# Layer 2 of a two-layer vision tower: the masked key copies of both halves of the heads on the scalar engine alone

## The chip, the cores and the metric

The kernel runs on one core of one Trainium2 chip. The time is device microseconds (us), the median of the runs. TensorE (PE), VectorE (DVE), the scalar engine (ACT), GpSimd (POOL) and the DMA queues (SP issues most of them) run side by side, each with its own instruction stream in program order, and meet at semaphores.

## The reference

The input is 32 images of 96 x 96 x 3. Patches of 16 x 16 become 36 tokens of 192 features, and a class token makes 37. Then come four blocks, each followed by a residual sum and a layer norm: attention with 12 heads of 16 features; a soft mixture of 64 experts; a second attention with two score maps; a second expert block. The change is in the second attention alone:

```
q = (x @ Wq).reshape(B, N, 2, H, D)      # 2 maps, 12 heads of 16
k = (x @ Wk).reshape(B, N, 2, H, D)
v = (x @ Wv).reshape(B, N, H, D)
out = softmax(q0 k0 / 4) v - exp(lambda) * softmax(q1 k1 / 4) v
h = layernorm(h + out @ Wo + bo)
```

## The kernel before, in words

**Tiling.** The 32 images go through the attention in four steps, called quads here: 8 images each, as 4 pairs (`QP = 4`, `QUADS = 4`). A pair lies on 101 partitions: one image on rows 0 to 36, the other on rows 64 to 100. The 192 features lie in two halves of 96 (`FH`), six heads each (`HH`). Times of 444 us to 640 us of the profiled execution are the second attention: quad 0 to about 495 us, quad 1 to 541, quad 2 to 587, quad 3 after that.

**Why there are masked copies.** For one pair, one map and one half, the scores of six heads come from one product: the stationary side is q of the half (96 features x 37 tokens), the moving side is K with 6 x 37 columns. So that a column belongs to one head alone, K is stored six times, each time with the features of all other heads put to zero. This masked copy is `k * hmask[:, h]`, read from PSUM, 96 partitions x 296 elements (8 images x 37 tokens) into `k_heads`. A quad of the second attention has 2 maps (m), 2 halves (mc) and 6 heads: 24 copies. The half mc = 0 is copied by ACT in `act_q` (L447), the half mc = 1 by VectorE in `dve_k` (L457), 12 copies each in every quad.

**What PE does in a quad** (`step` of `l1_pe`, L885). First q and K of map 1 (`pe_qk`, L353) into banks 4 to 7, for which it waits until the residual of the quad before (L961) has read banks 4 and 5. Then V (`pe_v`, L370) into banks 2 and 3. K of map 0 stood there, so `pe_v` waits for the copies of map 0. Then `pe_attention`: for each of eight units u (4 pairs x 2 maps), scores (L388), a turn of the probabilities (L399) and the product with V (L415); the first scores (u = 0) wait for all 24 masked copies. Between unit 0 and unit 1 it turns the normed output of the quad before (L880). Then, for the next quad, the turn of its input (L334), and of this quad's output (L552); q and K of map 0 of the next quad (L353, banks 0 to 3), and last the output projection of this quad (L905).

**What ACT does.** `act_q(1)`: two copies of q (L442) and the masked K of map 1; then for each unit the exp (L490) and the copy of turned probabilities (L497); copies of turned tiles (L344, L560); and `act_q(0)` of the next quad.

**What VectorE does** (`l1_dve`, L922). `dve_k` of map 1, the scaling of the layer norm of the quad before (`ln_scale`, L579), then per unit the row maximum (L480), the subtraction (L485) and the normalising (L520 to L533); the V copies (L474) between unit 1 and unit 2. At the quad's end `start(it + 1)`: its part of the turned input (L344) and `dve_k` of map 0 of the next quad; then the residual (L961, one piece for each half of the projection), and the moments of the norm (L571, L574), from which GpSimd makes the inverse deviation (L586).

**Order.** The order on each engine is as written in these functions. `maps` is 1 in the first layer and 2 in the second; `act_q`, `dve_k` and `pe_scores` serve both.

Of the kernel before, what the change touches and what calls it, by code (L numbers as in the profile page):

```python
# [13 lines left out]
B, T, D = 32, 37, 192  # L14
# [4 lines left out]
HH = NH // 2  # L19
FH = D // 2  # L20
# [9 lines left out]
QT = QB * T  # L30
# [18 lines left out]
def tower(nc, io):  # L49
# [3 lines left out]
    ACT = mybir.ActivationFunctionType  # L53
# [3 lines left out]
    def spread(ap, axis, n):  # L57

        ap = ap.unsqueeze(axis)
        shape = list(ap.shape)  # L60
        shape[axis] = n
        return ap.to_broadcast(shape)

    def nth(step, per, n):

        return step * per + n
# [6 lines left out]
    with ExitStack() as ctx:  # L73
        def sb(name, shape, dt=f32):
            return ctx.enter_context(nc.sbuf_tensor(name, shape, dt))
# [16 lines left out]
        def tenant(home, rows, at, shape, dt=f32):  # L92
            n = 1
            for x in shape:
                n *= x
            words = n // (2 if dt == bf16 else 1)
            ap = home[0:rows, at:at + words]
            if dt != f32:
                ap = ap.bitcast(dt)
            names = "abcde"[:len(shape)]  # L100
            kw = {c: x for c, x in zip(names, shape)}
            return ap.rearrange(f"p ({' '.join(names)}) -> p {' '.join(names)}", **kw)
# [28 lines left out]
        k_heads1 = tenant(stream, FH, 12 * D, [2, 2, QB, HH, T])  # L131
# [13 lines left out]
        hmask = sb("hmask", [FH, HH])  # L145
# [28 lines left out]
        bias_km = sb("bias_km", [FH, 2, HH])  # L174
# [93 lines left out]
        P = ctx.enter_context(nc.psum_tensor("P", [128, 8, 512], f32))  # L268
# [24 lines left out]
        def layer_sems(p, *names):  # L293
            return {n: sem(f"{p}_{n}") for n in " ".join(names).split()}
# [62 lines left out]
        def v_bank(maps):  # L357

            return 6 if maps == 1 else 2

        def pe_v(pe, L, it, maps, w_v):

            if maps == 2:

                pe.wait_ge(L["k_ready_a"], nth(it, HH * maps, HH))
                pe.wait_ge(L["k_ready_v"], nth(it, HH * maps, HH))
            for b in range(QB):
                for e in range(2):
                    for kc in range(2):
                        mm = pe.matmul(P[64 * e:64 * e + T, v_bank(maps) + b // 4, (b % 4) * FH:(b % 4 + 1) * FH],  # L370
                                       h_t[:, kc, b, :], w_v[:, kc, e * FH:(e + 1) * FH],
                                       start=(kc == 0), stop=(kc == 1), skip_group_check=True)
                if b % 4 == 3:
                    mm.then_inc(L["v_made"], 1)

        def pe_scores(pe, L, it, maps, u, k_heads):
            j, m = u // maps, u % maps
            if u == 0:
                pe.wait_ge(L["q_ready"], nth(it, 2 * maps, 2 * maps))
                pe.wait_ge(L["k_ready_a"], nth(it, HH * maps, HH * maps))  # L380
                pe.wait_ge(L["k_ready_v"], nth(it, HH * maps, HH * maps))
            if u >= 2:

                pe.wait_ge(L["shifted"], nth(it, QP * maps, u - 1))
            for e in range(2):
                b = 2 * j + e
                for mc in range(2):
                    mm = pe.matmul(P[64 * e:64 * e + T, u % 2, mc * HH * T:(mc + 1) * HH * T],  # L388
                                   q_t[:, m, mc, b * T:(b + 1) * T], k_heads[:, m, mc, b, :, :],
                                   start=True, stop=True, skip_group_check=True)  # L390
            mm.then_inc(L["scores"], 1)
# [28 lines left out]
        def pe_attention(pe, L, it, maps, k_heads, after_first=None, before_turn=None, beside_mix=None):  # L420
# [3 lines left out]
            for k in range(U + 2):  # L424
# [8 lines left out]
                if k >= 2:  # L433
                    pe_mix(pe, L, it, maps, k - 2)
                    if beside_mix and k - 2 < QP:
                        beside_mix(k - 2)

        def act_q(act, L, it, maps, which, bias, k_heads):
            for m in which:
                for mc in range(2):  # L440
                    act.wait_ge(L["q_made"], nth(it, 2 * maps, 2 * m + mc + 1))
                    act.activation(q_t[:, m, mc, :], P[0:FH, 4 * m + mc, 0:QT], ACT.Identity,  # L442
                                   bias=0.0 if bias is None else bias[:, mc:mc + 1]).then_inc(L["q_ready"], 1)
                act.wait_ge(L["k_made"], nth(it, 2 * maps, 2 * m + 1))
                for h in range(HH):

                    act.activation(k_heads[:, m, 0, :, h, :], P[0:FH, 4 * m + 2, 0:QT].rearrange("p (b t) -> p b t", t=T),  # L447
                                   ACT.Identity, scale=hmask[:, h:h + 1],
                                   bias=0.0 if bias is None else bias_km[:, 0, h:h + 1]).then_inc(L["k_ready_a"], 1)

        def dve_k(dve, L, it, maps, which, bias, k_heads):
            for m in which:
                dve.wait_ge(L["k_made"], nth(it, 2 * maps, 2 * m + 2))
                for h in range(HH):
                    src = P[0:FH, 4 * m + 3, 0:QT].rearrange("p (b t) -> p b t", t=T)
                    if bias is None:
                        ins = dve.tensor_scalar(k_heads[:, m, 1, :, h, :], src, hmask[:, h:h + 1], None, ALU.mult)  # L457
                    else:
                        ins = dve.tensor_scalar(k_heads[:, m, 1, :, h, :], src, hmask[:, h:h + 1],
                                                bias_km[:, 1, h:h + 1], ALU.mult, ALU.add)  # L460
                    ins.then_inc(L["k_ready_v"], 1)
# [167 lines left out]
        L1 = layer_sems("l1", TURN, ATTENTION, "mapped")  # L629
# [292 lines left out]
        def l1_dve(dve):  # L922
            def combined(quad, j):

                dve.wait_ge(s_mix, nth(quad, QP, j + 1))
                dve.tensor_tensor(xn[0:ROWS, j:j + 1, :], P[0:ROWS, 2 + j % 2, MIX:MIX + D].unsqueeze(1),
                                  h1_all[0:ROWS, ds(quad * QP + j, 1), :], ALU.add).then_inc(L0["resid"], 1)

            def start(quad):
                take_turned(dve, dve.tensor_copy, L1, quad, 1, h_t)  # L930
                dve_k(dve, L1, quad, 2, (0,), None, k_heads1)

            def step(it, first, last):
                dve_k(dve, L1, it, 2, (1,), None, k_heads1)
                if not first:

                    ln_scale(dve, LO, it - 1, attn, h_out)
                def with_bias():
                    if not first:

                        dve.wait_ge(s_h3, it)
                    dve.tensor_tensor(h_out[0:ROWS, :, :], h_in[0:ROWS, :, :], spread(rowc[0:ROWS, 4, :], 1, QP),
                                      ALU.add).then_inc(s_hb, 1)
                between = {1: lambda: dve_v(dve, L1, it, 2, False), 7: with_bias}
                if not first:
                    between[0] = lambda: take_x3(dve, dve.tensor_copy, it - 1, 1)
                if not last:
                    def scale():
                        dve.wait_ge(s_hb, nth(it, 1, 1))
                        ln_scale(dve, L0, it + (QUADS + 1), xn, h_in)  # L950

                    between.update({k + 2: lambda k=k: combined(it + 1, k) for k in range(QP)})
                    between[6] = lambda: ln_moments(dve, L0, it + (QUADS + 1), xn)
                    between[8] = scale
                dve_attention(dve, L1, it, 2, between)
                if not last:
                    start(it + 1)
                dve.wait_ge(s_hb, nth(it, 1, 1))
                for g in range(2):
                    dve.wait_ge(s_wo, nth(it, 2, g + 1))  # L960
                    dve.tensor_tensor(attn[0:ROWS, 2 * g:2 * g + 2, :], P[0:ROWS, 4 + g, 0:2 * D].rearrange("p (j d) -> p j d", j=2),  # L961
                                      h_out[0:ROWS, 2 * g:2 * g + 2, :], ALU.add).then_inc(LO["resid"], 2)
                ln_moments(dve, LO, it, attn)

            dve.wait_ge(s_lam, 1)
            for j in range(QP):
                combined(0, j)
            ln_moments(dve, L0, QUADS, xn)
            ln_scale(dve, L0, QUADS, xn, h_in)
            start(0)  # L970
            steps(dve, step)
            ln_scale(dve, LO, QUADS - 1, attn, h_out)
            take_x3(dve, dve.tensor_copy, QUADS - 1, 1)
# [132 lines left out]
        def l0_pe(pe):  # L1106
# [68 lines left out]

            start(0)
            pe_v(pe, L0, 0, 1, w_v0)
            l0_steps(pe, step)

# [636 lines left out]
```

## Time and profile before

| what | value |
|---|---|
| median of 3 runs | 1026.44 us (1025.55 to 1026.45) |
| time of the profiled execution | 1035.84 us |
| its span, first to last instruction | 1033.9 us |
| PE busy in the span | 819.7 us (79%) |
| DVE busy | 563.3 us (54%) |
| ACT busy | 367.6 us (36%) |
| mean granted clock of PE | 0.814 |

The page of a profile lists each engine's busy time, the chain of work that ended last (followed back from the last instruction, at each step to what released it), and groups of instructions by line. The timeline merges neighbouring instructions of one kind: its first two numbers are the start and the length of the run of instructions, and the bracket at the end says how long the engine was idle before and who released it. The clock is the share of full speed that PE was granted: 1.00 is 2.4 GHz and 0.50 is 1.2 GHz.

### The profile page before, as it was taken

The page shows a single profiled execution, that of the slowest core. Times are in us where ns is not written, and L with a number is a line of the kernel's source. Part 1 is how long each engine was busy: PE and PEld are TensorE (multiplying, and loading weights), DVE is VectorE, ACT ScalarE, POOL GpSimd, SP SyncE. Part 2 cuts the span into 40 slices and gives each one's busy share as a digit, 9 for nine tenths or more (in the row PEclk, how much of TensorE's full clock was granted, in tenths as well). Part 3 has the DMA queues.
Part 4 walks back from the last instruction along what each step waited for, and adds up shares of the span by engine and source line. Part 5 has one row for each costly group of instructions (what it writes and reads, how often), then busy time and mean ns, then how long its engine had stood idle before and what let it go on. Part 6 is the DMA issues. An engine that isn't in the chain of part 4 may idle for free.

```text
span 1033.9 us, 19679 instructions
## 1 busy us (share of the span) xinstructions
PE 819.7 (79%) x6882; PEld 470.5 (46%) x6882; DVE 563.3 (54%) x1563; ACT 367.6 (36%) x785; POOL 98.4 (10%) x133
## 2 busy tenths in 40 slices
PE   6899999849788786579988987433899899899930
PEld 4567676645433333356766665111333333333310
DVE  4465656540111111055586676988678587677850
ACT  0313122203211110032334342333678577677700
POOL 0020202022221200000001011232000000000010
PEclk9787869657977787785799898665899999999975
DMA  8410100004999999890000001632100000000000
GB/s 308 201 37 1 35 0 0 1 1 182 418 429 422 401 424 424 187 110 4 1 2 1 0 1 68 108 60 47 48 2 2 2 1 1 2 1 1 1 14 23
DMA packets 24855, 102.56 MB, mean 99 GB/s; under 512 B 3391, under 2 KB 14595, under 8 KB 20563
## 3 DMA queue, kind: packets, MB, share of 16 engines
q1 hardware_dynamic: 23734, 98.37, 28.1%
q0 software_dynamic: 1056, 3.44, 0.9%
q8 instruction: 27, 0.44, 0.2%
q14 instruction: 38, 0.31, 0.1%
HBM read 93.08 MB, written 5.07 MB: 95 GB/s over the span
## 4 chain that ended last, share of the span: by engine, by line
PE 62%; DMA 13%; DVE 13%; issue 6%; ACT 2%; POOL 1%; SPq 1%; DVEq 0%; ACTq 0%; POOLq 0%
DMA stream<-in_fc_dram 11%; PE P L1452 8%; PE P L1427 7%; PE P L1436 7%; PE P L353 6%; PE P L1101 5%; PE P L415 5%; PE P L388 4%; PE P L399 4%; PE P L769 3%; PE P L370 2%; PE P L1445 2%; DVE work L1569 2%; DMA out_dram<-work 1%; PE P L1170 1%
## 5 line engine op out<-in xcount | busy, mean ns | idle before, releaser
L1596 DVE TENSOR_TENSOR work<-work,P 128x396 f32<-128x396 f32 x384 | 193.1, 562 | 65.4 <-PE P L1436 45.1
L1523 ACT ACTIVATE work<-P 128x396 f32<-128x396 f32 x384 | 178.5, 500 | 57.2 <-PE P L1427 56.9
L1427 PE MATMUL P<-stream 99*128 x384 | 129.5, 340 | 12.4 <-ACT work L1523 10.6
L1436 PE MATMUL P<-early,middle 96*128 x384 | 129.8, 339 | 0.6 <-DVE work L1596 0.6
L1452 PE MATMUL P<-work 128*32 128x396 f32 x768 | 84.6, 508 | 0.0
L1427 PEld LDWEIGHTS P<-stream 99*128 99x128 bf16 x384 | 37.8, 98 | 100.7 <-ACT work L1523 54.2
L811 DVE COPY work<-P 128x768 f32<-128x768 f32 x16 | 15.3, 958 | 97.2 <-PE P L759 97.2
L584 POOL TENSOR_SCALAR work<-work 101x4 f32<-101x4 f32 x16 | 3.7, 229 | 672.8 <-DVE work L574 672.8
L796 ACT ACTIVATE work<-P 128x768 f32<-128x768 f32 x16 | 13.0, 812 | 153.7 <-PE P L751 153.7
L490 ACT ACTIVATE work<-work 101x444 f32<-101x444 f32 x48 | 28.1, 585 | 104.0 <-DVE work L485 104.0
L1101 PE MATMUL P<-early 128*37 128x192 f32 x384 | 54.3, 363 | 10.0 <-DMA early<-in_patches_dram 7.0
L415 PE MATMUL P<-work 101*37 101x34 f32 x1152 | 57.3, 233 | 2.3 <-DVE work L474 2.3
L399 PE MATMUL P<-ident,work 101*128 101x101 f32 x288 | 47.6, 319 | 13.0 <-ACT work L490 10.4
L415 PEld LDWEIGHTS P<-work 101*37 101x37 f32 x1152 | 52.4, 149 | 9.7 <-issue 7.6
L1436 PEld LDWEIGHTS P<-early,middle 96*128 96x128 bf16 x384 | 37.8, 98 | 35.4 <-DVE work L1596 17.4
L399 PEld LDWEIGHTS P<-ident,work 101*128 101x128 f32 x288 | 35.8, 179 | 33.6 <-issue 20.5
L769 PE MATMUL P<-stream,work 128*32 128x192 f32 x768 | 48.4, 419 | 3.2 <-DVE work L811 3.2
L1101 PEld LDWEIGHTS P<-early 128*37 128x37 f32 x384 | 37.1, 127 | 26.1 <-issue 10.4
L816 DVE COPY work<-P 128x192 f32<-128x192 f32 x16 | 5.7, 358 | 77.7 <-PE P L769 77.7
L353 PE MATMUL P<-work,stream 96*96 96x296 f32 x128 | 40.0, 475 | 4.1 <-DVE work L961 3.5
L480 DVE TENSOR_REDUCE work<-P 101x12 f32<-101x444 f32 x48 | 29.6, 617 | 22.4 <-PE P L388 22.1
L457 DVE TENSOR_SCALAR stream<-P,hmask 96x296 f32<-96x296 f32 x48 | 21.5, 515 | 35.6 <-PE P L353 35.6
(210 smaller groups left out, 1231.1 us busy)
## 6 DMA issues: line engine op xcount, KB each, us to landing
stream<-in_fc_dram SPq DMA_DIRECT2D x16, 2304.0 KB
stream<-in_fc_dram SPq DMA_DIRECT2D x16, 1536.0 KB, 17.5
stream<-in_fc_dram SPq DMA_DIRECT2D x16, 768.0 KB, 19.0
early<-stream SPq DMA_DIRECT2D x36, 99.0 KB, 2.3
early<-in_patches_dram SPq DMA_DIRECT2D x4, 888.0 KB, 5.1
stream<-w_dram SPq DMA_DIRECT2D x6, 512.0 KB
work<-in_w_dram SPq DMA_DIRECT2D x1, 2048.0 KB, 8.2
stream<-z_dram SPq DMA_DIRECT2D x6, 297.0 KB, 10.0
```

Source lines behind the costliest of these rows:

```text
L353: mm = pe.matmul(P[0:FH, at + mc, 0:QT], w[:, kc, m * D + mc * FH:m * D + (mc + 1) * FH], h_t[:, kc, :, :], start=(kc == 0), stop=(kc == 1))
L388: mm = pe.matmul(P[64 * e:64 * e + T, u % 2, mc * HH * T:(mc + 1) * HH * T], q_t[:, m, mc, b * T:(b + 1) * T], k_heads[:, m, mc, b, :, :], ...
L399: mm = pe.transpose(P[:, 4 + 2 * (u % 2) + hp // 3, (hp % 3) * ROWS:(hp % 3 + 1) * ROWS], probs[0:ROWS, u % 2, hp, :, :].rearrange("p a k ...
L415: mm = pe.matmul(P[64 * e:64 * e + T, 2 + u % 2, hp * w2:(hp + 1) * w2], probs_t[0:ROWS, u % 2, hp, 64 * e:64 * e + T], v_blk[0:ROWS, 2 * ...
L480: dve.tensor_reduce(row_max[0:ROWS, u % 2, :], src, AX, ALU.max).then_inc(L["row_max"], 1)
L769: mm = pe.matmul(P[32 * j:32 * j + B, 6 + u, 0:D], hidden_t[:, u, c, B * j:B * (j + 1)], fc2[:, u, c, j, :], start=False, stop=(c == HC - ...
L1101: mm = pe.matmul(P[64 * e:64 * e + T, 2 + j // 2, (j % 2) * D:(j % 2 + 1) * D], patches[:, c, 2 * j + e, :], w_patch[:, c, :], start=(c == ...
L1427: pe.matmul(P[:, n % 3, 0:TC], w1s[:, seg, i * 128:(i + 1) * 128], zs[:, seg, ds(it * TC, TC)], start=True, stop=True).then_inc(s_u1, 1)
L1436: pe.matmul(P[:, 3 + n % 3, 0:TC], gate_sel[:, c, :], ws[:, 2 * seg + hh, ds(it * TC, TC)], start=True, stop=True).then_inc(s_bc, 1)
L1452: pe.matmul(P[32 * j:32 * j + 32, 6 + sq, 0:TC], w2[:, i, seg, :], gated[:, n % 8, :], start=False, stop=(hh == 1 and c == CH // 2 - 1), s ...
L1523: act.activation(act_out[:, n % 4, :], P[:, n % 3, 0:TC], ACT.Gelu_apprx_tanh).then_inc(s_ua, 1)
L1596: dve.tensor_tensor(gated[:, n % 8, :], act_out[:, n % 4, :], P[:, 3 + n % 3, 0:TC], ALU.mult).then_inc(s_ug, 1)
```

## The change

In the second layer, ACT makes the masked copies of both halves and VectorE makes none. `act_q` now goes through mc = 0 and mc = 1, each after its own K product; with `DVE_HEADS = {1: HH, 2: 0}` the first layer keeps six copies of the second half on VectorE. The two calls of `dve_k` in `l1_dve` are gone. The waits of `pe_v` and `pe_scores` count up to 12 and 24 copies of ACT in the second layer and nothing of VectorE.

```diff
@@ pe_v
-                pe.wait_ge(L["k_ready_a"], nth(it, HH * maps, HH))
-                pe.wait_ge(L["k_ready_v"], nth(it, HH * maps, HH))
+                pe.wait_ge(L["k_ready_a"], nth(it, (2 * HH - DVE_HEADS[maps]) * maps, 2 * HH - DVE_HEADS[maps]))
@@ pe_scores
-                pe.wait_ge(L["k_ready_a"], nth(it, HH * maps, HH * maps))
-                pe.wait_ge(L["k_ready_v"], nth(it, HH * maps, HH * maps))
+                pe.wait_ge(L["k_ready_a"], nth(it, (2 * HH - DVE_HEADS[maps]) * maps, (2 * HH - DVE_HEADS[maps]) * maps))
+                if maps == 1:
+                    pe.wait_ge(L["k_ready_v"], nth(it, HH, HH))
@@ act_q
+        DVE_HEADS = {1: HH, 2: 0}
...
-                act.wait_ge(L["k_made"], nth(it, 2 * maps, 2 * m + 1))
-                for h in range(HH):
-
-                    act.activation(k_heads[:, m, 0, :, h, :], P[0:FH, 4 * m + 2, 0:QT].rearrange("p (b t) -> p b t", t=T),
-                                   ACT.Identity, scale=hmask[:, h:h + 1],
-                                   bias=0.0 if bias is None else bias_km[:, 0, h:h + 1]).then_inc(L["k_ready_a"], 1)
+                for mc in range(2):
+                    act.wait_ge(L["k_made"], nth(it, 2 * maps, 2 * m + mc + 1))
+                    for h in range(HH if mc == 0 else HH - DVE_HEADS[maps]):
+
+                        act.activation(k_heads[:, m, mc, :, h, :],
+                                       P[0:FH, 4 * m + 2 + mc, 0:QT].rearrange("p (b t) -> p b t", t=T),
+                                       ACT.Identity, scale=hmask[:, h:h + 1],
+                                       bias=0.0 if bias is None else bias_km[:, mc, h:h + 1]).then_inc(L["k_ready_a"], 1)
@@ l1_dve
             def start(quad):
                 take_turned(dve, dve.tensor_copy, L1, quad, 1, h_t)
-                dve_k(dve, L1, quad, 2, (0,), None, k_heads1)
 
             def step(it, first, last):
-                dve_k(dve, L1, it, 2, (1,), None, k_heads1)
```

On ACT, at the head of the second layer (quad 0), the rows before are these: the turned input, q of map 0, its copies of K (`stream`), q of map 1, its copies, and the first exps.

```order
75 L344 COPY work<-P 96x2x74 x2
76 L442 ACTIVATE work<-P 96x296 x2
77 L447 ACTIVATE stream<-P,hmask 96x8x37 x6
78 L442 ACTIVATE work<-P 96x296 x2
79 L447 ACTIVATE stream<-P,hmask 96x8x37 x6
80 L490 ACTIVATE work<-work 101x12x37 x2
```

After the change the same place holds the following (L444, L450 and L494 are the lines that were L442, L447 and L490).

```order
75 L344 COPY work<-P 96x2x74 x2
76 L444 ACTIVATE work<-P 96x296 x2
77 L450 ACTIVATE stream<-P,hmask 96x8x37 x12
78 L444 ACTIVATE work<-P 96x296 x2
79 L450 ACTIVATE stream<-P,hmask 96x8x37 x12
80 L494 ACTIVATE work<-work 101x12x37 x2
```

Both runs of six have become runs of twelve, and q of map 1 stands behind the first twelve. On VectorE, from the end of quad 0 into quad 1, the rows before are: the turned input, the copies of map 0, the residual, the moments, the loop's head, the copies of map 1, the norm's scaling, and the first unit's maximum.

```order
245 L344 COPY work<-P 96x2x74 x2
246 L457 TENSOR_SCALAR stream<-P,hmask 96x8x37 x6
247 L961 TENSOR_TENSOR work<-P,work 101x384 x2
248 L571 BN_STATS work<-work 101x6 x4
249 L574 BN_AGGR work<-work 101x2 x4
250 L863 UNCONDITIONAL_BRANCH
251 L863 ISA
252 L457 TENSOR_SCALAR stream<-P,hmask 96x8x37 x6
253 L579 TENSOR_SCALAR work<-work 101x192 x4
254 L479 ISA
255 L480 TENSOR_REDUCE work<-P 101x12
```

After the change (L963 was L961, L575 and L578 were L571 and L574, L583 was L579, L484 was L480):

```order
244 L344 COPY work<-P 96x2x74 x2
245 L963 TENSOR_TENSOR work<-P,work 101x384 x2
246 L575 BN_STATS work<-work 101x6 x4
247 L578 BN_AGGR work<-work 101x2 x4
248 L867 UNCONDITIONAL_BRANCH
249 L583 TENSOR_SCALAR work<-work 101x192 x4
250 L483 ISA
251 L484 TENSOR_REDUCE work<-P 101x12
```

The residual now stands directly behind the turned input, and the scaling directly behind the moments. PE's own order is unchanged.

## Rows read from the trace of the kernel before

**Rows 1.** The page: share of each engine in the chain that ended last.
```profile
PE 62%; DMA 13%; DVE 13%; issue 6%; ACT 2%; POOL 1%; SPq 1%; DVEq 0%; ACTq 0%; POOLq 0%
```

**Rows 2.** Chain of waits in order of time, quads 0 and 1: start, length, what.
```profile
456.47 2.80 PE P L370 x64
...
459.35 0.97 PE P L388 x8
...
462.24 0.14 issue
462.38 0.71 PE P L399 x6
463.09 0.89 PE P L388 x8
463.98 1.18 PE P L399 x6
...
467.54 1.64 PE P L388 x8
...
503.84 2.62 DVE stream L457 x6
506.46 1.00 DVE work L961 x2
...
507.59 4.22 PE P L353 x16
511.82 2.80 PE P L370 x64
...
514.69 0.95 PE P L388 x8
```

**Rows 3.** Timeline of quad 0, ACT and VectorE: the copies of K and q.
```profile
451.53 2.48 ACT L447 ACTIVATE stream<-P,hmask 96x296 f32<-96x296 f32 x6 [0.59 <-PE P L353]
452.52 2.69 DVE L457 TENSOR_SCALAR stream<-P,hmask 96x296 f32<-96x296 f32 x6 [6.30 <-PE P L353]
453.88 0.42 ACT L442 ACTIVATE work<-P 96x296 f32<-96x296 f32 x1
...
455.51 2.48 ACT L447 ACTIVATE stream<-P,hmask 96x296 f32<-96x296 f32 x6 [0.58 <-PE P L353]
```

**Rows 4.** Groups by form, ACT, 440 to 640 us: busy us, mean ns of one.
```profile
L447 ACT ACTIVATE stream<-P,hmask 96x296 f32<-96x296 f32 x48 | 19.8, 505 | 4.7 <-PE P L353 4.7
```

**Rows 5.** Timeline, quad 0 to quad 1: PE's projection, and ACT's copies.
```profile
503.64 2.76 PE L905 MATMUL P<-stream,work 96*101 96x192 f32 x16
...
502.84 2.48 ACT L447 ACTIVATE stream<-P,hmask 96x296 f32<-96x296 f32 x6 [0.59 <-PE P L353]
508.86 0.41 ACT L442 ACTIVATE work<-P 96x296 f32<-96x296 f32 x1 [3.54 <-PE P L353]
...
510.86 2.48 ACT L447 ACTIVATE stream<-P,hmask 96x296 f32<-96x296 f32 x6 [0.58 <-PE P L353]
```

**Rows 6.** Timeline, end of quad 3, where no `dve_k` precedes the residual.
```profile
630.83 2.77 PE L905 MATMUL P<-stream,work 96*101 96x192 f32 x16
...
632.43 0.56 DVE L961 TENSOR_TENSOR work<-P,work 101x384 f32<-101x384 f32 x1 [1.87 <-PE P L905]
633.70 0.56 DVE L961 TENSOR_TENSOR work<-P,work 101x384 f32<-101x384 f32 x1 [0.71 <-PE P L905]
```

**Rows 7.** Stretches: PE, PEld, DVE, ACT, POOL busy, then clock, DMA share, GB/s.
```profile
458.00:462.00 4.00, 2.98 (x47) 2.14 (x42) 2.83 (x6) 0.35 (x1) 0.00 (x0) 1.00 1.02 116
462.00:466.00 4.00, 3.60 (x37) 2.76 (x38) 3.81 (x8) 1.37 (x3) 0.00 (x0) 0.75 0.52 58
466.00:470.00 4.00, 4.00 (x28) 2.42 (x24) 2.08 (x7) 1.14 (x2) 0.00 (x0) 0.50 0.06 20
...
459.35:495.09 35.74, 34.40 (x312) 24.27 (x312) 23.22 (x64) 9.23 (x16) 1.27 (x2) 0.56 0.15 19
514.69:541.20 26.51, 22.90 (x320) 16.67 (x320) 23.70 (x69) 9.57 (x18) 3.54 (x4) 0.96 0.01 2
```

## Prediction

> **What bounds the kernel now.** I read the chain of waits on the page first: PE holds 62% of it, VectorE and DMA 13% each, ACT 2% [rows 1]. So PE's order sets the time, and a change to ACT or VectorE counts only where PE waits for it. Then I read the same chain in order of time through the second attention [rows 2]. The reader is to see two kinds of place. The first is the entry to the scores: V products (L370), then scores (L388), almost without a gap. In quad 0 V ends at 456.47 + 2.80 = 459.27 and the scores start at 459.35; in quad 1, 514.62 and 514.69. The second is the hand-over between quads: PE's projection ends at 503.64 + 2.76 = 506.40 [rows 5], VectorE's six copies end at 506.46, two residual sums end at 507.46, and PE begins q and K of map 1 at 507.59 [rows 2]. This hand-over occurs three times, since quad 3 has no follower. The timelines of ACT and VectorE [rows 3, 5] then say when copies start and end beside PE.
>
> Both engines' copies now finish just inside PE's V products: in quad 0 ACT's last run ends at 455.51 + 2.48 = 457.99 [rows 3], VectorE's run begins about a microsecond after ACT's and takes 2.69. So ACT has a slack of 459.35 − 457.99 = 1.4 us, and VectorE almost none. Twelve copies in a row don't fit into that slack, so the end of ACT's run becomes what the scores wait for.
>
> **Price of a copy.** Six copies take 2.48 us [rows 3] and one takes 505 ns [rows 4], so the next starts (2.48 − 0.505) / 5 = 0.395 us after the last. Twelve take 11 × 0.395 + 0.505 = 4.85 us. The six that are added have the same shape and kinds of operands as the six that stand there, only other banks, so I put the same price on them. VectorE's price per copy is 2.69 / 6 = 0.45, so ACT isn't slower for one copy; the loss is that two runs side by side become one run twice as long. From ACT's end to PE's start I take 0.14 us, as between exp and turn at 462.24 [rows 2].
>
> The Trainium skill ("ScalarE: Activation LUTs", What ACT_TABLE_LOAD costs) has an ACTIVATE with immediates at 186 ns + 0.833 ns an element, 93 ns more for each pointer operand, and an overlap of 93 ns back to back: for 296 elements and a pointer scale 0.526 us, and one every 0.433. The trace has 0.505 and 0.395, so it is a little under both. By the page twelve would take 5.29 us instead of 4.85, and the whole would be 4 × 0.44 = 1.8 us more; the measured price decides.
>
> **Quad 0.** Map 0: ACT starts at 451.53. Its seventh copy would start at 451.53 + 6 × 0.395 = 453.90; the product that it reads is there, because VectorE began on it at 452.52 [rows 3]. The twelfth ends at 456.38. V now waits for it: 456.38 + 0.14 = 456.52 against 456.47. That is 0.05 us, and the wait that replaces it below hides it. Map 1: the q copies follow at 456.25 (they overlap the last K copy by 0.13, as 453.88 stands against 454.01 now) and take about 0.29 each, so K starts at 456.83 and ends at 461.68. Scores start at 461.82 against 459.35: **+2.47 us**.
>
> **Quads 1 to 3.** First a gain. The residual no longer queues behind six copies. Where nothing queues in front (end of quad 3), the second residual sum starts 633.70 − 630.83 = 2.87 us after the projection's start and takes 0.56 [rows 6]. From 503.64 it would end at 507.07, and with the same 0.13 as now PE begins at 507.20 and not 507.59: −0.39. The 2.62 us of copies that the chain shows there give back only this, because the projection itself ends at 506.40: PE is late next. ACT's longer run for map 0 ends at 502.84 + 4.85 = 507.69 and is covered: the first q of map 1 comes 1.27 us after PE's start (508.86 against 507.59), now at 508.47. V's wait for it is met long before 511.4.
>
> Then the loss. K of map 1 starts on ACT 510.86 − 507.59 = 3.27 us after PE's start [rows 2, 5]. With twelve copies and the release, scores start 3.27 + 4.85 + 0.14 = 8.26 us after PE's start; now it is 514.69 − 507.59 = 7.10. So +1.16 − 0.39 = +0.77 per quad, **+2.3 us** for three.
>
> What VectorE gains otherwise: its twelve copies fewer per quad are 48 × 0.44 = 21 us of its time, all in places where it then waits for PE. The norm's scaling (L579) moves forward into that idle time. Softmax of unit 0 starts when the scores are there, after as before. GpSimd's part is earlier too and covered. I take nothing for these. The order of the eight units stays as it is relative to the first scores. No DMA and no instruction on GpSimd or SP is added or moved; the count of ACT's instructions per quad rises by twelve, VectorE's falls by twelve.
>
> **Clock in quad 0.** PE ran at 1.00 (2.4 GHz) when the scores began, and the stretch 462 to 466 has 0.75, the next 0.50 (1.2 GHz) [rows 7]: it fell at about 464. Before that PE had stood idle between its second scores and 462.38, some 1.3 us. It then stayed at the lower level for the rest of the quad. With the change an idle time of 461.82 − 459.3 = 2.5 us comes first, and the same 1.3 us after the second scores. So I expect it at the lower level no later than now, while the work is 2.47 us later. The turn of unit 0 would start at 464.85 and the scores of unit 2 behind it: 1.18 + 1.64 instead of 0.71 + 0.89 us [rows 2], **+1.2 us**. This term is the least certain: the bounds are 0 (the level falls just as late after the work) and the whole difference between softmax stages at the two levels, below. I take 1.2, as the row of the fall is nearest.
>
> **Sum.** 2.47 + 2.3 + 1.2 = +6.0 us on the profiled execution, 1035.84 to 1041.8. Its span and time differ by 1.9 us, which this leaves alone. The median is 9.4 us under the profiled time; I add the same 6.0 to it: 1026.44 + 6.0 = **1032.4 us**.
>
> **Rivals.**
>
> *A whole stage more at the lower clock (slower still).* The stage from first scores to the quad's end takes 35.74 us in quad 0 at clock 0.56 and 26.51 in quad 1 at 0.96 [rows 7]: 9.2 us. The unprofiled runs are 9.4 us faster than the profiled one. If the reason is that quad 0 stays at 2.4 GHz in most of them, then the new idle time of 2.5 us drops it there and the cost is 2.47 + 2.3 + 9.2 + 1 = 15, 1041.4. The same 9.2 would come from a fall in one of quads 1 to 3, where PE now idles some 1.2 us before the scores and didn't before. Against: three runs within 0.9 us show no sign of two levels, and in quads 1 to 3 the idle time at the residual shrinks by 0.4. Chance 0.20. The Trainium skill ("TensorE: Matmul & The Clock Gate", A second HAM failure mode) describes a PE that micro-idles between groups and swings between the two levels; the fall at 464 agrees, and that page speaks for this rival.
>
> *The chain taken at its word (not slower).* The copies stand in the chain at the three hand-overs with 2.62 us each [rows 2]. If all of it went, −7.9 us, against 2.47 + 3 × 1.16 = +6.0: 1024.5, faster by 0.19%. It decides if the residual could start at 503.84; the projection that it adds ends only at 506.40 [rows 5], which speaks against it. Chance 0.03.
>
> *The clock holds in quad 0 (faster).* If the later start of the scores falls so that PE keeps 2.4 GHz through quad 0, 9.2 us go and 4.8 come: 1022.0. It needs less idle time before 464, and there is more. Chance 0.04.
>
> *ACT's time is hidden (no change).* If the level rises one step earlier at the start of each quad because q and K start at another moment, or quad 0's fall costs nothing, the sum lies at 2 us or below: 1028. The bound from below is the three gains alone, −1.2 us, 1025.3. Chance 0.07.
>
> *The copies don't behave as priced.* If ACT's copies of the second half cost more (another bank while PE writes), 1 to 2 us on top; that lies within my own range.
>
> **How the numbers follow.** Forecast 0.66, at 1032.4, its own range 1030 to 1035. Range for 8 in 10: 1028.6 to 1041.5; it reaches into the first rival. What a measurement can tell from no change is about 0.2%, 2 us: 1024.4 to 1028.5. Faster 0.05, within 0.08, slower 0.87.
>
> **What the profile after would show.** ACT's copies in runs of twelve of about 4.85 us; the scores of unit 0 released by ACT and not following V at once; PE idle before them 2.4 us in quad 0 and about 1.2 in quads 1 to 3. The residual directly after the projection, PE's wait for it at 0.8 us instead of 1.19. Runs shorter than 4.6 us, or scores that still follow V, would prove the price wrong. A clock of 0.5 in the softmax stage of quads 1 to 3 is the first rival; of 1.0 in quad 0, the third.

## The result, and the profile after

The changed kernel takes 1047.83 us (median of 4 runs, 1044.45 to 1049.16) against 1026.45 us (4 runs, 1025.55 to 1028.46): 1.0181 times as long, 95% interval 1.0153 to 1.0209. In a second comparison on one chip it took 1047.43 against 1029.07 us, ratio 1.0165 (1.0143 to 1.0188). Its first profiled execution has a span of 1042.5 us; that of before has 1033.9. The two traces thus differ by 8.6 us, the medians by 21.4. Of the 8.6, the second attention (first turn to the next block's first product) has 5.6: 195.67 us before, 201.25 after.

The chain by engine comes first. Against [rows 1] ACT has risen from 2% to 4%, PE fallen from 62% to 60%.

```profile
PE 60%; DMA 13%; DVE 12%; issue 6%; ACT 4%; POOL 1%; SPq 1%; DVEq 0%; ACTq 0%; POOLq 0%
```

The chain in order of time, quad 0 and the start of quad 1, answers to [rows 2] (L450 are ACT's copies of K, L444 those of q, L963 the residual):

```profile
452.10 4.86 ACT stream L450 x12
456.95 0.60 ACT work L444 x2
457.56 4.75 ACT stream L450 x12
462.31 0.14 issue
462.44 0.97 PE P L388 x8
...
465.34 0.14 issue
465.47 1.24 PE P L399 x6
466.71 1.64 PE P L388 x8
468.36 1.21 PE P L399 x6
469.56 1.43 PE P L415 x24
...
510.62 0.57 DVE work L963
511.19 0.12 issue
511.31 3.24 PE P L353 x12
514.58 1.06 ACT stream L450 x3
515.64 0.13 issue
515.77 3.68 ACT stream L450 x9
519.44 0.04 issue
519.49 0.95 PE P L388 x8
```

The reader is to see that in quad 0 PE's products of V and the last ones of K have left the chain, and that ACT's runs of twelve stand there. PE's own timeline shows the idle time in its brackets, in quad 0 and at both ends of the hand-over:

```profile
457.00 2.87 PE L369 MATMUL P<-stream,work 96*37 96x96 f32 x64
462.44 1.71 PE L388 MATMUL P<-stream,work 96*37 96x222 f32 x16 [2.57 <-ACT stream L450]
465.47 1.24 PE L399 MATMUL P<-ident,work 101*128 101x101 f32 x6 [1.32 <-ACT work L494]
...
511.31 4.22 PE L353 MATMUL P<-work,stream 96*96 96x296 f32 x16 [0.80 <-DVE work L963]
...
519.49 0.95 PE L388 MATMUL P<-stream,work 96*37 96x222 f32 x8 [1.15 <-ACT stream L450]
```

The last view is of stretches, as in [rows 7]: three of 4 us around the fall of the clock, then from the first scores to the quad's end for quads 0 and 1.

```profile
458.00:462.00 4.00, 1.87 (x46) 1.66 (x41) 0.00 (x0) 4.00 (x11) 0.00 (x0) 1.00 1.08 124
462.00:466.00 4.00, 2.23 (x19) 1.64 (x20) 2.49 (x5) 0.96 (x3) 0.00 (x0) 0.80 0.68 76
466.00:470.00 4.00, 4.00 (x27) 2.49 (x26) 3.26 (x6) 1.47 (x3) 0.00 (x0) 0.50 0.05 20
...
462.44:499.44 37.00, 35.67 (x313) 24.91 (x313) 23.22 (x64) 9.36 (x16) 1.27 (x2) 0.53 0.08 11
519.49:546.66 27.17, 23.57 (x320) 17.16 (x320) 23.16 (x66) 9.57 (x18) 1.27 (x2) 0.93 0.01 2
```

Quad 0's softmax stage ran at 1.2 GHz and took 37.0 us. In the trace of before it ran there too (35.7 us). So the two traces agree on what most timed runs don't: from the experiments I conclude that in the kernel before that stage usually keeps 2.4 GHz and takes about 25 us. No trace of such a run of before exists; the nearest is the kernel below with the change in quads 1 to 3 alone, whose quad 0 has before's split of the copies (25.31 us at 0.99).

### The profile page after: what moved, and what is told of

Its sections match the earlier page's. It is cut to its first block, busy times and chain, and to the rows that moved or that the text cites. A ratio compares the mean times of both kernels' runs of the same rounds, so it can differ in the third digit from the quotient of the medians.

```text
span 1042.5 us, 19678 instructions
## 1 busy us (share of the span) xinstructions
PE 824.0 (79%) x6882; PEld 472.0 (45%) x6882; DVE 542.5 (52%) x1515; ACT 386.8 (37%) x833; POOL 98.6 (9%) x133
## 4 chain that ended last, share of the span: by engine, by line
PE 60%; DMA 13%; DVE 12%; issue 6%; ACT 4%; POOL 1%; SPq 1%; DVEq 0%; ACTq 0%; POOLq 0%
DMA stream<-in_fc_dram 11%; PE P L1454 7%; PE P L1429 7%; PE P L1438 7%; PE P L1103 5%; PE P L353 5%; PE P L415 4%; PE P L399 4%; PE P L388 4%; PE P L773 3%; ACT stream L450 2%; PE P L1447 2%; DVE work L1571 2%; DMA out_dram<-work 1%; PE P L1172 1%
## 5 line engine op out<-in xcount | busy, mean ns | idle before, releaser
L494 ACT ACTIVATE work<-work 101x444 f32<-101x444 f32 x48 | 28.1, 586 | 99.6 <-DVE work L489 99.6
L484 DVE TENSOR_REDUCE work<-P 101x12 f32<-101x444 f32 x48 | 29.6, 617 | 53.2 <-PE P L388 52.9
L353 PE MATMUL P<-work,stream 96*96 96x296 f32 x128 | 39.1, 467 | 2.9 <-DVE work L963 2.3
L388 PE MATMUL P<-stream,work 96*37 96x222 f32 x256 | 35.8, 398 | 6.1 <-ACT stream L450 6.1
```

The source lines that it names most:

```text
L353: mm = pe.matmul(P[0:FH, at + mc, 0:QT], w[:, kc, m * D + mc * FH:m * D + (mc + 1) * FH], h_t[:, kc, :, :], start=(kc == 0), stop=(kc == 1))
L484: dve.tensor_reduce(row_max[0:ROWS, u % 2, :], src, AX, ALU.max).then_inc(L["row_max"], 1)
```

## The experiments

Theory A: the longer copy runs cost their plain wait, some 5 us, and the rest is PE's clock in quad 0, which the new idle time lets fall for a whole softmax stage. The rivals: the loss is spread over the quads, lies outside the second attention, or hangs on who makes the copies. Four groups of kernels ran, each group with its own runs of the kernel before.

| kernel | its median | before | ratio (95%) | softmax stage of quad 0, clock (one trace) |
|---|---|---|---|---|
| the change again | 1047.43 | 1029.07 | 1.0165 (1.0143 to 1.0188) | 37.19, 0.51 |
| filled behind V | 1038.09 | 1029.07 | 1.0098 (1.0064 to 1.0132) | 25.75, 0.97 |
| map 0 alone | 1028.32 | 1029.07 | 0.9987 (0.9976 to 0.9999) | 26.27, 0.94 |
| map 1 alone | 1045.31 | 1029.07 | 1.0082 (1.0036 to 1.0127) | 25.18, 1.00 |
| quad 0 alone | 1043.18 | 1029.35 | 1.0137 (1.0103 to 1.0170) | 37.02, 0.53 |
| quads 1 to 3 alone | 1031.26 | 1029.35 | 1.0018 (0.9997 to 1.0039) | 25.31, 0.99 |
| filled at two places | 1036.53 | 1029.35 | 1.0068 (1.0042 to 1.0093) | 26.52, 0.92 |
| map 0, with fillings | 1023.30 | 1029.35 | 0.9926 (0.9897 to 0.9955) | 25.18, 1.00 |
| idle time alone | 1044.35 | 1029.37 | 1.0142 (1.0127 to 1.0158) | 37.77, 0.50 |
| idle time, filled | 1030.28 | 1029.37 | 1.0012 (0.9999 to 1.0026) | 26.50, 0.92 |
| fillings alone | 1024.63 | 1029.37 | 0.9947 (0.9934 to 0.9961) | 25.17, 1.00 |
| tiny products on VectorE | 1044.99 | 1028.80 | 1.0151 (1.0117 to 1.0186) | 37.76, 0.50 |

**The change again.** No edit.

> The changed kernel once more, to read its own spans and granted clocks beside those of the kernel before on the same chip. Theory A (longer copy run, +6 us, and the rest is PE at the lower clock): +18 to +22 us; the trace shows the twelve-copy runs of 4.9 us, and the mean clock times span gives 10 to 15 us more at 1.2 GHz than before. Theory B (something outside the second attention grew): the stretch 444 to 640 us grows by under 7 us and the others by the remainder.

It came out at +18.4 us. The second attention, from its first turn (L334) to the next block's first product (L1386), took 203.00 us in this trace. Its low stage is like that of the first one. Mean clock over the span in its five runs was 0.805 to 0.811, in the 23 runs of before 0.817 to 0.829. With two levels, 1.00 and 0.50, the time at the lower one is twice (1 − clock) times the span: 401 us on average against 365, so some 36 us more are spent at 1.2 GHz. That is about one softmax stage at the lower level (37.19 at 0.51). I had put it at 10 to 15 us more, which is what such a stage gets longer by; but all of its 37 us then count as low. Theory B can't be read off the stretch 444 to 640 us, since the only trace of before has the low stage too.

**Which part of the change.** Two kernels with half of it by map, two with half of it by quad (their edit of `act_q` in short, against the changed kernel):

```diff
# map 0 alone (map 1 alone: m == 1)
-                for mc in range(2):
+                for mc in range(2 if maps == 2 and m == 0 else 1):
# quad 0 alone (quads 1 to 3 alone: it != 0)
+                for mc in range(2 if L is L1 and it == 0 else 1):
# VectorE calls dve_k for the others; the counts of pe_v and pe_scores match
```

> Half of the change: ACT makes both halves for map 0 only (the copies that stood in front of the residual on VectorE); map 1 stays split. Theory A: no idle time is added before the scores; 3 x 0.39 us are gained at the residual, about 0.1 lost in quad 0: 1025.4, -1 us. Rival: the loss sits in map 0 (the wait of V or the order of q behind twelve copies): +2 us or more.

> The other half: ACT makes both halves for map 1 only; map 0 stays split, and VectorE's copies still stand before the residual. Theory A: scores are late by about 1.2 us in each of four quads, +5 us, plus the clock: an idle time of 1.2 us more before the scores of quad 0 instead of 2.5, so the sum is between +5 and +16. Rival (the clock falls only for the idle time of 2.5 us): +5 to +6.

Map 0 alone takes 0.75 us less than before (interval −0.1 to −2.5), near A's −1: nothing is lost. Map 1 alone idles PE 1.20 us before the first scores in place of 2.57. Its twelve runs fall into two groups: four at 1029.9 to 1031.4 us with mean clocks of 0.819 to 0.825, eight at 1044.4 to 1046.3 us with 0.803 to 0.812. The ratio, which leaves out the five longest of them, stands for neither. The trace is of the first group, so that the second group's extra time lies in quad 0 is concluded from its clocks and its size of 15 us, not seen. The rival's +5 to +6 is nowhere. A's range doesn't fit well either: the lower group is +0.9 to +2.3, the upper +15.4 to +17.2 against the kernel before.

> The change in quad 0 alone: ACT makes all 24 copies of quad 0, quads 1 to 3 are split as before. Theory A (the cost is quad 0's softmax stage at the lower clock): +2.5 us for the longer run and +11 to +13 for the clock, so +13 to +16 us, nearly all of the change's cost; the trace has PE at 0.5 from shortly after the first scores to the end of quad 0. Rival (the cost is spread over the four quads): +4 to +6 us.

> The change in quads 1 to 3 alone; quad 0 is split as before. Theory A: +2.3 us (3 x 0.77), the clock of quad 0's softmax stage holds as often as in the kernel before. Rival (spread): +12 us or more.

Quad 0 alone costs 13.8 us, quads 1 to 3 alone 1.9 us (interval −0.3 to +4.0). The loss isn't spread. The 1.9 isn't the attention's waits alone: this kernel also has the longer stretch behind the second attention that the last experiment is about. These are the stages from first scores to the end of quad 0; first the kernel with the change in quad 0 alone:

```profile
464.50:501.52 37.02, 35.69 (x312) 24.92 (x312) 23.22 (x64) 9.37 (x16) 1.27 (x2) 0.53 0.06 9
```

and the kernel with the change in quads 1 to 3:

```profile
459.52:484.83 25.31, 21.39 (x312) 15.60 (x313) 21.69 (x61) 9.23 (x16) 1.27 (x2) 0.99 0.20 26
```

Same instructions, PE busy nearly all the time at the lower level (35.69 of 37.02) and 21.39 us at the upper: 11.7 us of stage for the clock.

**Idle time without the change.** ACT writes nine copies again before those that count, in quad 0; the split between the engines stays as before.

```diff
+                again = (3, 6) if (L is L1 and it == 0 and m == 1) else ()
+                for n in again:
+                    for h in range(n):
+                        act.activation(k_heads[:, m, 0, :, h, :], ...)   # the same copy
+                    # and ACT waits for these n
                 for h in range(HH):
```

> The kernel before with nothing moved between engines; only ACT makes nine further copies of K in quad 0 (map 1, first half, written again with the same values) before the six that count, so PE waits some 2.4 us for it before the first scores of quad 0, as in the changed kernel. Theory A (the idle time of PE there lets the clock fall for the whole softmax stage): +13 to +15 us, as for the change in quad 0 alone; softmax stage of quad 0 at 37 us. Rival (the fall hangs on which engine makes the copies, or on VectorE being idle): +2.5 to +3 us.

+15.0 us, and PE waited 2.66 us before the scores:

```profile
466.12 3.18 PE L388 MATMUL P<-stream,work 96*37 96x222 f32 x16 [2.66 <-ACT stream L455]
```

Nothing moved between engines here, so the rival (who copies) falls.

**The same idle time, filled.** To that kernel, products that nobody reads:

```diff
+                for k in range(4 if first else 0):          # behind pe_v
+                    pe.matmul(P[0:FH, k % 2, 0:QT], ident[0:FH, 0:FH], h_t[:, 0, :, :], start=True, stop=True)
+                # and 2 of them into bank 7 behind the scores of unit 1, in quad 0
```

> The same with the idle time of PE in quad 0 filled with unread products (4 behind V, 2 behind the scores of unit 1); the scores still wait for ACT. Theory A: the clock holds and only the plain wait is left, +2.5 to +3.5 us. Rival (the late release itself costs, whatever PE does meanwhile): +13 us or more.

+0.9 us, 14 less than unfilled, though the scores are late here too. In PE's timeline of this kernel (L905 the first filling, L435 the second) they start at 461.66, 17.83 us after the second attention's first turn; in the trace of before it is 15.27 (459.35 in [rows 2], the turn at 444.08).

```profile
456.11 2.87 PE L370 MATMUL P<-stream,work 96*37 96x96 f32 x64
458.91 2.23 PE L905 MATMUL P<-work,ident 96*96 96x296 f32 x8
461.66 1.71 PE L388 MATMUL P<-stream,work 96*37 96x222 f32 x16 [0.51 <-issue]
463.29 1.24 PE L435 MATMUL P<-work,ident 96*96 96x296 f32 x4
```

The stages of quad 0 in the pair, first idle, then filled (each from its own trace):

```profile
466.12:503.89 37.77, 37.17 (x313) 25.58 (x313) 23.30 (x64) 9.29 (x16) 1.27 (x2) 0.50 0.02 5
```

```profile
461.66:488.16 26.50, 23.78 (x316) 17.28 (x317) 22.61 (x64) 9.24 (x16) 1.27 (x2) 0.92 0.10 14
```

The first kernel adds to before only the wait ahead of the first scores, and costs 15.0 us; the second keeps that wait and gives PE something to do in it and behind the scores of unit 1, and 14.1 come back. So the added idle time costs its 11 us of stage through the clock. The pair doesn't say how much of the cure each of the two fillings has. The net of 0.9 is under the expected 2.5 to 3.5 (the interval of the ratio ends at +2.7), and why stays open; one of its eleven runs took 1036.41 us.

**The changed kernel, filled.** The same fillings on the changed kernel: behind V alone (4 in quad 0, 2 in the others), then also behind the scores of unit 1 in quad 0.

> The changed kernel with idle PE filled: after V, PE makes products that nobody reads (ident x turned input, 296 columns, into banks 0 and 1), 4 in quad 0 (about 2.1 us at full clock) and 2 in quads 1 to 3 (about 1.05 us). The scores still wait for ACT's twelfth copy. Theory A (clock): the level of PE holds through more of the softmax stages, so the time falls well under the changed kernel's, to between before + 4.5 and before + 10 us, or under before if quad 0 holds. Theory B (plain waits): no change against the changed kernel, or up to 1 us slower.

> The changed kernel with PE filled at two places: unread products behind V (4 in quad 0, 2 in the others), and 2 more in quad 0 behind the scores of unit 1, where PE idles about 1.3 us. Theory A: quad 0's softmax stage holds 2.4 GHz in nearly every run: +4.8 to +6 us on the kernel before, the plain price of the longer runs. If the runs still fall at times as in the kernel with the first filling alone (1035 to 1045 us), the idle time behind the scores wasn't what let the clock fall there.

The first gives back 9.3 us, with runs from 1035.35 to 1045.46 us: two of six (1043.54 and 1045.46, clocks 0.813 and 0.806) look as if the level had fallen. With the second gap filled, six runs lie between 1035.99 and 1038.51. That points to the 1.3 us behind the scores taking part in the fall, but two of six against none of six doesn't show it. At +7.2 it is a microsecond above the expected range; the last experiment bears on that.

**A version that beats both.** Map 0 on ACT, and fillings where PE idles: 2 behind the scores of unit 1 in quad 0, and in every quad 1 before the turn of unit 6 and 3 before that of unit 7.

```diff
+                    n, bank = {1: (2 if is_first else 0, 7), U - 1: (1, 4), U: (3, 0)}.get(k, (0, 0))
+                    for _ in range(n):
+                        pe.matmul(P[0:FH, bank, 0:QT], ident[0:FH, 0:FH], h_t[:, 0, :, :], start=True, stop=True)
                 if 1 <= k <= U:
                     pe_turn_probs(pe, L, it, maps, k - 1)
```

> A version meant to beat both: ACT makes both halves for map 0 only, and PE is filled with unread products where it idles: 2 behind the scores of unit 1 in quad 0, and in every quad 1 before the turn of unit 6 and 3 before the turn of unit 7, where the trace of the kernel before has the clock fall at the end of quads 1 and 2. Theory A: quad 0 never falls and each quad's end keeps 2.4 GHz through the turns and the products of q and K, which took 7 to 10 us at 1.2 GHz: 8 to 12 us faster than before. Rival (the fills delay PE by what they win, or the clock falls from another idle time): within 2 us of before.

1023.30 us, 6.1 under the kernel before (ratio 0.9926, 0.9897 to 0.9955) and 24 under the changed one. In its trace PE keeps the upper level from quad 0's first scores to the end of quad 3's softmax stage. Its quad 1, from the first scores to the quad's end, against 26.51 at 0.96 in [rows 7]:

```profile
506.11:531.95 25.84, 24.43 (x330) 17.11 (x329) 23.09 (x67) 9.57 (x18) 3.54 (x4) 1.00 0.01 2
```

The gain is below the 8 to 12 expected. One part of that is seen: quad 3, which had kept 1.00 without fillings (22.32 us), takes 23.63 with them.

> The kernel before with the fillings of the faster version alone (2 in quad 0 behind the scores of unit 1; 1 before the turn of unit 6 and 3 before that of unit 7 in every quad), and its split of the copies as before. Theory A: the gain of the faster version is the clock's, 4 to 6 us of it here, and about 1 us is the residual's. Rival (ACT's copies of map 0 carry it): under 2 us.

1024.63 us, 4.7 under before. The fillings carry the gain. Map 0 on ACT adds 1.3 us by the two differences, which their intervals don't tell from nothing.

**What lies behind the second attention.** From the next block's first product to the end the trace takes 394.15 us before and 396.51 after, though the change doesn't touch it. It is 396.5 to 396.7 in all five traces of kernels that lack VectorE's copies for both maps in quads 1 to 3, and 393.7 to 394.9 in the eight others. The last kernel gives VectorE its instructions back:

```diff
+            for h in range(HH):      # where dve_k stood, twice a quad
+                dve.tensor_scalar(rmx[0:FH, 3 * m + h // 2, h % 2:h % 2 + 1], hmask[:, h:h + 1], hmask[:, h:h + 1], None, ALU.mult)
...              # and, ahead of the loop, dve_k's waits
```

> The changed kernel with VectorE's instruction count restored: where its copies of K stood it waits as before and makes six products of one element each (hmask by hmask, read by nobody). In all profiles of kernels in which VectorE's copies are gone from both places of quads 1 to 3, what lies after the second attention takes some 2 us more, mostly in the expert loop, which the change doesn't touch. Theory C (the place of VectorE's later code in its instruction stream): that part falls back to 394 to 395 us from 396.5, and the time to about 2 us under the changed kernel, +15 to +17 us. Rival (something else): it stays at 396.5, and the time within 1 us of the changed kernel's or above it.

In its trace that part has fallen back. The whole is +16.2 us, inside the expected range; but its ratio (1.0151) and the changed kernel's (1.0165) have intervals that overlap, so the trace alone carries this. The same stretch, of the changed kernel and of this one:

```profile
645.99:1042.50 396.51, 294.45 (x1756) 115.60 (x1756) 280.25 (x760) 214.86 (x459) 27.42 (x29) 0.83 0.11 25
```

```profile
651.78:1044.70 392.92, 290.07 (x1756) 113.96 (x1756) 280.58 (x760) 214.79 (x459) 27.40 (x29) 0.83 0.11 25
```

So 2 to 3 us go with VectorE's instructions standing there or not. How that costs time in later code stays open. The place of that code in the stream (theory C) is not shown: the tiny products also bring back `dve_k`'s waits and some work for VectorE, and nothing about how code is fetched was measured.

## Why the prediction was wrong

**The price of a copy** was right: twelve in 4.86 us (quad 0, map 0), where [rows 3] have six in 2.48, against 4.85 forecast. The estimate from the figures of the Trainium skill ("ScalarE: Activation LUTs", What ACT_TABLE_LOAD costs) was 5.29; the trace decides for the lower one.

**Quad 0's wait** was right: PE idle 2.57 us before the scores, where it was 0.08 in the trace of before; forecast +2.47. **Quads 1 to 3** were right: PE's wait at the residual 0.80 (forecast 0.8), idle time before the scores 1.15, 1.15 and 1.24 (forecast about 1.2). By these waits the forecast of 2.3 us for the three quads stands; the 1.9 us of the kernel with these quads alone can't confirm it, because it holds the longer stretch behind the attention as well. PE kept the upper level for nearly all of these stages: their clocks are 0.93, 0.94 and 1.00 after the change, 0.96, 0.93 and 1.00 before. The rival that took the chain at its word fell with this: the copies gave back 0.39 of their 2.62 us.

**The clock in quad 0** is the step that failed, and with it the carrying of the same 6.0 us from the profiled execution to the median. The term was taken as +1.2 us, because in the profiled execution of before the level had fallen at 464 already. Between the two traces it came out so: the stage grew from 35.74 to 37.00 us, and the second attention by 5.6 against the sum of 6.0. But that execution (1035.84 us) wasn't like the timed ones (median 1026.44), and the 9.4 us between them stood in the table. Over all comparisons, 62 of the 65 timed runs of before lie between 1025.5 and 1032.1 us, the other three between 1035.2 and 1036.3. By these times and by the trace of 25.31 us above, before's timed runs keep 2.4 GHz there as a rule. All nine timed runs of the changed kernel lie at 1044 us or more, and both of its traces have the low stage. The step should have read: stage of quad 0 at the upper level 25.2 to 26.3 us, at the lower one 37.0 to 37.2, so +11 to +12. With 2.5 and 2.3 that makes 16 to 17, and the 2 to 3 us of the stretch behind bring it to 18 to 20; measured are 17.0 (by the ratio 1.0165) to 21.4.

**The first rival** was that very case, with a chance of 0.20 and a price of 15. Its price was too low for two reasons. It compared quad 0 with quad 1 (26.51), which turns the normed output besides and has a lower level at its end: 9.2 in place of 11 to 12. And no term stood for the stretch behind the attention, which neither the sum nor any rival had. Its argument against itself, that three runs within 0.9 us show no two levels, was the mistake in reading: they showed one level, the other one. Of a clock that holds in quad 0 the prediction said that it needs less idle time, and there was more: it held in neither trace.

The Trainium skill ("TensorE: Matmul & The Clock Gate", A second HAM failure mode) has a PE that micro-idles between groups of products swing between the two levels. The traces agree in that the level here goes down and up again more than once (after the change 0.50 in quad 0, 1.00 from 506 us on, 0.93 over quad 1's stage), and the pair with the same wait idle and filled, 1044.35 and 1030.28 us, shows that idle time of a few microseconds decides it. Inside quad 0 there is one fall and no return.

## What to carry to other kernels

Before adding up waits, compare the profiled execution's time with the median; where they differ by the size of one stage at 1.2 against 2.4 GHz, price the stage at both levels and ask which of them the timed runs have. Idle time that the change gives PE next to idle time that it has already is the place to look, and a few unread products there tell with one more kernel whether the clock is the cost. Moving work off VectorE gains only what PE waited for it, here 0.39 us of 2.62.

## What the runs showed that I had not expected

Once at 1.2 GHz, PE stayed there for the rest of quad 0 while it was busy 35.67 of 37.00 us with turns, small products and scores; it came back only during the products of q and K of the next quad (L353, from 502.16 on), as the clocks 0.65 and 1.00 of these two stretches of the trace after show:

```profile
504.00:506.00 2.00, 2.00 (x6) 1.18 (x5) 0.00 (x0) 0.45 (x2) 0.00 (x0) 0.65 0.00 0
506.00:508.00 2.00, 2.00 (x10) 1.39 (x9) 0.00 (x0) 1.42 (x4) 0.00 (x0) 1.00 0.00 0
```

So 1 to 3 us of idle time decide over 11. With 1.20 us before the scores (map 1 alone) it fell in eight runs of twelve, by their times; with the 2.57 and 2.16 us of the changed kernel's two traces, in all nine.

Unread products pay for themselves: four to six fp32 products of 296 columns a quad made this kernel, whose chain is PE for 62%, 4.7 us faster.

With VectorE's copies gone from one block, a later, unchanged stretch took 2 to 3 us longer (five traces against eight), and with twelve tiny products and their waits per quad in their place it didn't (one trace).
